# A recommendation tower on one core: row numbers in 3 KB pieces, dense inputs in two transfers, and another order of look-ups

## The reference, cut to what matters

```python
# B=2048 rows, S=16 tables, F=39 fields, D=K=H=16; tables have 1000 to 125000 rows of 16 values
e = stack([tbl_s[ids[:, s]] for s in range(16)], axis=1)               # (2048, 16, 16), look-ups
A  = repeat(r_x0, 16, axis=1)                                          # (2048, 624, 16)
Bm = repeat(e, 39, axis=2).reshape(2048, 624, 16)
z  = einsum('bnh,bnd,nk,khd,kd->bkh', A, Bm, alpha, w, hv).reshape(2048, 256)
h  = concatenate([z, dense_ctx], 1)                                    # dense_ctx (2048, 16)
h  = maximum(h @ W_top1 + b_top1, 0)                                   # 512 wide
h  = maximum(h @ W_top2 + b_top2, 0)                                   # 256 wide
y  = h @ W_top3                                                        # (2048, 1)
```

## Time and profile before

| | us |
|---|---|
| median of 3 runs | 206.6 (205.4 to 207.29) |
| the profiled execution's own time | 207.42 |
| its span in the profile | 205.3 |
| its mean granted PE clock | 0.933 of full speed |

### The profile page before, as it was taken

How to read it: one execution, slowest core, us unless ns; L and a number is a source line. 1 busy time by engine, 2 the same in 40 slices (tenths; PEclk the granted TensorE clock), 3 DMA queues, 4 the chain that set the end, 5 groups by cost and what they waited for, 6 DMA issues and landing times.

```text
span 205.3 us, 5116 instructions
## 1 busy us (share of the span) xinstructions
PE 167.3 (81%) x2170; PEld 123.8 (60%) x2170; DVE 154.7 (75%) x207; ACT 65.5 (32%) x203; POOL 110.4 (54%) x119
## 2 busy tenths in 40 slices
PE   0446993337667999999968999997899899899983
PEld 0446993334354866777746667775577467477671
DVE  3597699159999898998798959888989595595000
ACT  2790018502401136118111451271117318311322
POOL 4777778777777777777777777777500000000000
PEclk9995599556997999999999999999999999999999
DMA  5645589999967999960589999209721960000000
GB/s 123 180 113 131 140 210 224 200 252 203 238 142 155 178 214 182 212 121 10 108 153 211 186 205 188 55 6 200 167 61 38 228 145 2 0 3 0 3 0 2
DMA packets 14098, 26.63 MB, mean 130 GB/s; under 512 B 3932, under 2 KB 11100, under 8 KB 12028
## 3 DMA queue, kind: packets, MB, share of 16 engines
q1 hardware_dynamic: 10156, 25.22, 56.2%
q0 software_dynamic: 3632, 1.06, 4.9%
q10 hardware_dynamic: 288, 0.04, 0.1%
HBM read 26.26 MB, written 0.05 MB: 128 GB/s over the span
## 4 chain that ended last, share of the span: by engine, by line
PE 51%; DVE 21%; DMA 15%; issue 6%; SPq 4%; ACT 1%; DVEq 0%
PE bank L678 15%; DVE prod L585 14%; PE bank L699 13%; PE bank L709 12%; DMA low_h<-low_dram 12%; PE bank L634 5%; DVE onehot L531 4%; PE bank L668 3%; PE bank L693 2%; DMA low_dram<-low 2%; SPq L304 2%; DVE picked L543 2%; DMA prod<-ids_d 1%; SPq L305 1%; DVE prod L487 1%
## 5 line engine op out<-in xcount | busy, mean ns | idle before, releaser
L340 POOL DMA_INDIRECT e_all<-tbl,ids_sb x112 | 109.0, 973 | 35.4 <-issue 33.9
L585 DVE TENSOR_TENSOR prod<-x_main,bank 128x2048 f32<-128x2048 f32 x32 | 72.1, 2278 | 9.2 <-issue 9.2
L678 PE MATMUL bank<-prod,coef 128*32 128x256 f32 x640 | 45.0, 397 | 9.2 <-DVE prod L585 8.5
L634 PE MATMUL bank<-parts,onehot 125*128 125x80 bf16 (+1 forms) x864 | 38.5, 210 | 12.1 <-DVE onehot L531 12.1
L634 PEld LDWEIGHTS bank<-parts,onehot 125*128 125x128 bf16 x864 | 36.4, 107 | 16.9 <-issue 14.9
L411 ACT ACTIVATE spread<-e_all 128x128 f32<-128x128 f32 (+3 forms) x128 | 29.0, 331 | 12.2 <-DMA e_all<-tbl,ids_sb 11.5
L678 PEld LDWEIGHTS bank<-prod,coef 128*32 128x32 f32 x640 | 17.3, 111 | 24.3 <-DVE prod L585 11.6
L699 PE MATMUL bank<-z_sb,w1z_sb 128*128 128x256 f32 x128 | 30.4, 380 | 0.0
L709 PE MATMUL bank<-h_sb,w_sb 128*128 128x256 f32 x128 | 29.8, 386 | 0.7 <-ACT h_sb L421 0.7
L531 DVE TENSOR_SCALAR onehot<-low_h,masks_sb 125x512 bf16<-125x512 f16 x72 | 23.2, 372 | 6.7 <-DMA low_h<-low_dram 6.7
L709 PEld LDWEIGHTS bank<-h_sb,w_sb 128*128 128x128 f32 x128 | 23.7, 190 | 6.9 <-ACT h_sb L421 3.1
(11 more groups left out here) (41 smaller groups left out, 66.1 us busy)
## 6 DMA issues: line engine op xcount, KB each, us to landing
x_main<-x_m SPq DMA_DIRECT2D x16, 512.0 KB, 8.9
x_last<-x_l SPq DMA_DIRECT2D x8, 1024.0 KB
low_h<-low_dram SPq DMA_DIRECT2D x12, 384.0 KB, 8.3
e_all<-tbl,ids_sb POOLq DMA_INDIRECT x112
x_last<-dense_t SPq DMA_DIRECT2D x8, 128.0 KB
prod<-small_tables SPq DMA_DIRECT2D x1, 672.0 KB, 6.3
w1z_sb<-w1z SPq DMA_DIRECT2D x1, 512.0 KB, 16.7
w_sb<-w SPq DMA_DIRECT2D x1, 512.0 KB, 17.1
```

The costliest lines, as they stand in the source:

```text
L340: pool.indirect_dma_start(out=e_all[:, t * E + s * D:t * E + (s + 1) * D], out_offset=None, in_=tables[s], in_offset=bass.IndirectOffsetOn ...
L585: dve.tensor_tensor(prod[:, c, :, :], x0[:, p, :, :], value_bank(g, c // 2)[:, c % 2 * GB:(c % 2 + 1) * GB].unsqueeze(1).broadcast_to([P, ...
L634: last = pe.matmul(look_ps[i % 2][:, t * w:(t + 1) * w], onehot[:, n, c, at:at + P], parts[:, part, col:col + w], start=(t == 0 and c == 0 ...
L678: last = pe.matmul(z_ps[p][32 * q:32 * q + 32, a * GB:(a + 1) * GB], coef[:, c, 4 * a + q, :], prod[:, c, 4 * a + q, :], start=(c == 0 and ...
```

## The change

There are four edits. (1) low_dram is laid out by quarter, so that a transfer of three tables is one run of 3 KB for each partition in place of three of 1 KB; the ids that the digits come from are arranged on the host to match. (2) The twelve dense transfers are two, each of which repeats its source over four partition blocks. The wait for the first row numbers ahead of them is gone, and the row numbers of quarter 1 are issued ahead of x0_last of group 0. (3) Three tables' one-hots (PREFETCH) are made between the first and the second table split, and in the first nine units the one-hots run three ahead of the picks, behind each pick. (4) UNITS_AT is (0, 2, 1, 2, 1, 2, 1) in place of (2, 1, 1, 2, 1, 1, 1).

```diff
--- before.py
+++ after.py
@@ -99,8 +99,9 @@
 RUNS = spread_runs()
 FIRST_COLS = COL0[3]
 LAST_COEF_AT = (2, 4, 6, 8)
-
-UNITS_AT = (2, 1, 1, 2, 1, 1, 1)
+PREFETCH = 3
+
+UNITS_AT = (0, 2, 1, 2, 1, 2, 1)
 LAYER1_AT, LAYER2_AT = (0, 1), 2
 
 
@@ -172,7 +173,7 @@
         low_h = sb("low_h", [P, 2, NSMALL, QUARTER], F16)
         pick = sb("pick", [P, NSMALL * TILES, DMAX])
         picked = sb("picked", [P, 2, QT * DMAX * D])
-        low_dram = nc.dram_tensor("low_dram", [NSMALL, B], F16, kind="Internal").ap()
+        low_dram = nc.dram_tensor("low_dram", [4, NSMALL, QUARTER], F16, kind="Internal").ap()
         alpha_sb = sb("alpha_sb", [P, F8, K])
         w_hv_sb = sb("w_hv_sb", [P, K * H + K])
         wh_sb = sb("wh_sb", [P, K, H])
@@ -198,7 +199,8 @@
         ids_f = early(2 * NSMALL * TILES).rearrange("p (a c) -> p a c", a=2)
         high = early(4 * NSMALL * TILES).rearrange("p (i a c) -> p i a c", i=2, a=2)
 
-        dense_f = [x0_last[:, 1, :, :].rearrange("p h b -> p (h b)")[:, a * HALF:(a + 1) * HALF] for a in range(2)]
+        dense_stage = x0_last[:, 1, :, :].rearrange("p h b -> p (h b)")
+        dense_f = [dense_stage[:, a * HALF:(a + 1) * HALF] for a in range(2)]
         w1d_f = z_sb[:, 0, :, :].rearrange("p a b -> p (a b)")
 
 
@@ -264,7 +266,7 @@
         y_ready = sem("y_ready")
         stored = sem("stored")
 
-        PREP_LOADS, MLP_LOADS, DENSE_LOADS = 2, 4, 12
+        PREP_LOADS, MLP_LOADS, DENSE_LOADS = 2, 4, 2
 
         block = ctx.enter_context(nc.Block())
 
@@ -282,8 +284,9 @@
                 if u >= 2:
                     sp.wait_ge(onehot_ready, 2 * NSMALL * (u - 1))
                 for n in range(0, NSMALL, 3):
-                    sp.dma_start(low_h[:, u % 2, n:n + 3, :], low_dram[n:n + 3, u * QUARTER:(u + 1) * QUARTER].unsqueeze(0).broadcast_to(
-                        [P, 3, QUARTER])).then_inc(low_in[u % 2][n // 3], 16)
+                    sp.dma_start(low_h[:, u % 2, n:n + 3, :].rearrange("p n b -> p (n b)"),
+                                 low_dram[u, n:n + 3, :].rearrange("n b -> (n b)").unsqueeze(0).broadcast_to(
+                                     [P, 3 * QUARTER])).then_inc(low_in[u % 2][n // 3], 16)
 
             sp.wait_ge(low_stored, 16)
             load_low(0)
@@ -296,16 +299,11 @@
                 sp.dma_start(x0_last[:, p, :, :], x0_l[g].unsqueeze(1).broadcast_to(
                     [2 * 8, J, HP * GB])).then_inc(last_in[p], 16)
 
-            for n in range(NSMALL // 3):
-                sp.wait_ge(low_in[0][n], 16)
-            for q in range(4):
-                rows = slice(32 * q, 32 * q + 32)
-                for a in range(2):
-                    sp.dma_start(dense_f[a][rows, :], dense_t[:, a * HALF:(a + 1) * HALF]).then_inc(dense_in, 16)
-                sp.dma_start(w1d_f[rows, :], w1d).then_inc(dense_in, 16)
+            sp.dma_start(dense_stage, dense_t.unsqueeze(0).broadcast_to([4, 32, B])).then_inc(dense_in, 16)
+            sp.dma_start(w1d_f, w1d.unsqueeze(0).broadcast_to([4, 32, N1])).then_inc(dense_in, 16)
             load_main(0, 0)
+            load_low(1)
             load_last(0, 0)
-            load_low(1)
             load_main(1, 1)
             sp.dma_start(w1z_sb[:, :, :], w1z.rearrange("(a p) n -> p a n", p=P)).then_inc(mlp_in, 16)
             sp.dma_start(w2_sb[:, :, :], w2.rearrange("(a p) n -> p a n", p=P)).then_inc(mlp_in, 16)
@@ -384,7 +382,7 @@
                 last.then_inc(coef_done, 1)
 
             act.wait_ge(low_ready, 1)
-            act.dma_start(low_dram.rearrange("n b -> (n b)").rearrange("(p c) -> p c", p=P), low16[:, :]).then_inc(low_stored, 16)
+            act.dma_start(low_dram.rearrange("u n b -> (u n b)").rearrange("(p c) -> p c", p=P), low16[:, :]).then_inc(low_stored, 16)
             spread_weights()
             spread_sums()
 
@@ -557,14 +555,15 @@
             dve.wait_ge(table_in, 16)
             split_tables(0, slice(0, FIRST_COLS))
             dve.wait_ge(split_step, 4)
+            for n in range(PREFETCH):
+                make_onehot(n)
             split_tables(1, slice(FIRST_COLS, W))
-            make_onehot(0)
             dve.wait_ge(pick_ready, 1)
             dve.wait_ge(low_ready, 1)
             for n in range(NSMALL):
-                if n < NSMALL - 1:
-                    make_onehot(n + 1)
                 pick_rows(n)
+                if n + PREFETCH < NSMALL:
+                    make_onehot(n + PREFETCH)
             split_dense()
             for i in units_at(0):
                 make_onehot(i)
@@ -765,7 +764,7 @@
     rows_to = lambda a, n: _np.concatenate([a, _np.zeros((n - a.shape[0],) + a.shape[1:], a.dtype)], 0)
     arrays = {
         "ids": flat(ids.reshape(TILES, P, S).transpose(1, 0, 2)),
-        "ids_d": flat(_np.stack([flat(hot.T).reshape(P, NSMALL * TILES),
+        "ids_d": flat(_np.stack([hot.T.reshape(NSMALL, 4, QUARTER).transpose(1, 0, 2).reshape(P, NSMALL * TILES),
                                  hot.reshape(TILES, P, NSMALL).transpose(1, 2, 0).reshape(P, NSMALL * TILES)], 1)),
         **{f"tbl_{s}": flat(tables[f"tbl_{s}"]) for s in GATHERED},
         "x0_m": flat(x0[:, :, 0:FM]).reshape(GROUPS, 2 * FM, HP * GB),
```

## The result

The changed kernel takes 217.08 us against 206.94 for the one before (medians of 4 executions), a ratio of 1.050 (95% interval 1.040 to 1.060). The forecast was 204.3 and "faster" or "same"; the change made it 5% slower. The profiled execution took 219.35 us (span 217.2), 2.3 above its median. Executions in a second, slower state stand outside the ratios: this one is counted there (1.6% above the fastest), and so are, among others, one of e2_tiled at 250.0 us and one of e5_oldunits at 246.4, both with a mean granted clock of about 0.66.

The account below looks back on a forecast made before the run. The front was taken to wait for quarter 1's row numbers, with PE and DVE alternating as the bound behind it. The sum -5.9 + 1.05 + 0.55 + 1.0 + 1.0 = -2.3 us gave a 204.3 us median, range 200.8 to 207.0.

Parts of the forecast that it names:

- step 0: Front up to the first product: it would start at 38.7 in place of 44.60, with quarter 1's row numbers landed in time.
- the split beside the spread: DVE's dense split during ACT's first spread: 3.8 us, done at 37.7 and off the path.
- 3 KB runs: First row-number piece lands at 14.4 in place of 15.6; if the longer runs bring nothing, the sum is 1.2 us less.
- Edit 3 costs 0.7 us: DVE's new front order: last pick ends at 33.8 against 33.15, in spite of the earlier row numbers.
- Gain 5.9 us at step 0: The first product starts at 38.7 in place of 44.60.
- The steps give back 3.6 us: Losses from the new look-up spread: 1.05 and 0.55 in groups 0 and 1, 1.0 for each of two later pairs.
- Rival D: Group 0's gathers queue behind bulk DMA and delay ACT's first spread to about 40; sum +3.7, 210.3 us; chance 0.11.
- D's second half: Group 1's gathers, wanted by 51.4 for ACT's spread; each microsecond beyond is lost in full.
- Rival B: New look-up spread costs nothing in later groups and PE's clock is back early in front; 200.7 us; chance 0.20.
- C: PE's full clock comes 3 us later in front and step 0 runs longer at half clock; 206.7 us; chance 0.14.

Follow-up runs that it names:

- e2_tiled: The changed kernel with the dense inputs as two transfers of 128 distinct rows, tiled on the host; 204.58 us, ratio 0.991.
- e5_oldunits: The changed kernel with eight dense transfers and the earlier UNITS_AT (2, 1, 1, 2, 1, 1, 1); 198.77 us, ratio 0.968.
- a4: The changed kernel's two repeated dense transfers (leading dimension 4), with SP waits before and behind so only gathers run beside; 22.6 us from weights' issue to next issue.
- e1_eight: The changed kernel with the dense inputs in eight transfers of 32 partitions in place of two repeated ones; 202.73 us, ratio 0.981.
- e8_3kb: The kernel before with the 3 KB row numbers alone changed; 201.65 us, ratio 0.982.
- e9_repeat: The kernel before with its twelve dense transfers replaced by the two repeated ones, wait and order kept; 224.15 us in one execution.
- e6_oldfront: The changed kernel with eight dense transfers and the earlier front order of table split and one-hots on DVE; 203.56 us, ratio 0.989.
- e7_oldboth: The changed kernel with eight dense transfers, earlier DVE front order and earlier UNITS_AT, so only the transfers differ from the kernel before; 198.92 us, ratio 0.968.
- e4_wait: The changed kernel with SP's wait for the first three row-number transfers put back ahead of the repeated dense transfers; 222.96 us.
- e3_two: The changed kernel with the two dense transfers repeating a 64-row source twice (leading dimension 2); 218.73 us.

## Why the prediction was wrong

**The step that failed** is in the part on step 0: "4.72 MB at 221 GB/s", and "the dense values come to ACT sooner, which nobody waits for". Both took the two dense transfers at the rate of all 16 engines. They ran on four (a4), and took 34.6 us from issue to landing in the changed kernel. What SP queued behind them was late too: the longest transfer of row numbers landed 35.6 us after its issue, against 16.9. And somebody does wait: ACT's program has round_dense ahead of the first spread. I had named the cover (the split beside the spread) but not the price if it went. None of the three rivals was this. I had counted the edit as fewer issues of the same bytes and not asked how a transfer is shared out. The order rows showed only the destination, 128 partitions; the source's four by 32 stood in the diff.

The Trainium skill has the rule (DMA: Bandwidth & Descriptors, Why a DMA increments its semaphore by 16 and not by 1): a transfer gets the largest number of engines, up to 16, that divides the slowest dimension (of those larger than 1) of both sides, which is 4 here. The trace agrees: 25.6% and 25.0% of 16 engines with a leading 4, 12.6% with a leading 2, and 76.9% from 16 to 20 us with 128 rows, whose start and end lie in that stretch.

**With that step mended, the sum held, in part by luck.** The kernel with 128 distinct rows differs from the changed one in nothing else:

| step | forecast, us | two transfers of distinct rows, us |
|---|---|---|
| first row numbers, from the store's landing | 4.2 | 3.6 |
| last pick ends | 33.8 | 33.7 |
| first product, group 0 | 38.7 | 38.76 |
| first product, group 1 | 60.5 | 60.19 |
| contraction (1, 1) | 67.6 | 67.26 |
| first product, group 4 | 118.9 | 118.89 |
| contraction (5, 1) | 149.3 | 148.89 |
| time | 205.1 for the profiled one, 204.3 median | 204.74 and 204.58 |

The rows of the table's first products (DVE, kernel with distinct rows), against the earlier trace rows:

```profile
38.76 2.29 DVE L584 TENSOR_TENSOR prod<-x_main,bank 128x2048 f32<-128x2048 f32 x1 [1.25 <-PE bank L667]
...
60.19 2.27 DVE L584 TENSOR_TENSOR prod<-x_main,bank 128x2048 f32<-128x2048 f32 x1
...
118.89 2.29 DVE L584 TENSOR_TENSOR prod<-x_main,bank 128x2048 f32<-128x2048 f32 x1 [4.14 <-issue]
```

and of its contractions (PE), against the earlier trace rows:

```profile
67.26 1.07 PE L677 MATMUL bank<-prod,coef 128*32 128x256 f32 x16 [0.65 <-DVE prod L584]
```
```profile
148.89 1.07 PE L677 MATMUL bank<-prod,coef 128*32 128x256 f32 x16 [0.46 <-DVE prod L584]
```

In this kernel's own trace the first product comes 5.8 us sooner than before and the steps give back 3.2 (158.63 - 38.76 against 161.32 - 44.60), so 2.7 are left (204.74 against 207.42), where the forecast had 5.9, 3.6 and 2.3. By medians it is 1.6 us (204.58 against 206.21, ratio 0.991). Two agreements are better than the reasoning behind them. The last pick is on time because two misses cancel: look-up 2 began at 19.13, 1.5 sooner than the 20.6 of the prediction, and PE's granted clock was still at 0.50 from 24 to 28 us and 0.75 from 28 to 32, where the kernel before had 0.73 and 1.00. And group 4's first product falls on the forecast with a break of 1.24 us of PE in it (at 108 us), of the kind seen in e1_eight, which the forecast did not have.

Point by point:

- **3 KB runs** (taken as 1.2 us for the first piece): between 1.5 and 1.8. The bound of 13.9 was reached. The Trainium skill's rule that 512 B suffice for line rate (DMA: Bandwidth & Descriptors, Specifications), weighed in the prediction, is not borne out here: with the 3 KB runs alone changed (e8_3kb) the fastest piece took 3.8 us from issue to landing, against 5.4 and 5.2 in e9_repeat with 1 KB runs.
- **Edit 3 costs 0.7 us**: neither confirmed nor refuted. With 3 KB runs the last pick ended at 29.9, 31.8 and 33.0 in the three traces with the old order (e8_3kb, e6_oldfront, e7_oldboth), the latter two with PE standing still for 1.42 and 2.45 us in a look-up. With the new order it ended anywhere from 29.9 to 36.4, later the longer PE ran at half speed in the front. In e4_wait, the latest, eight coefficient matmuls at 30.49 still took 1.87 us; at 28.59 in the changed kernel, the earliest, they took 1.04. (In e4_wait PEclk reads 1.00 there, so the length of the rows is the better witness.)
- **Gain 5.9 us at step 0**: 5.8 (44.60 to 38.76).
- **The steps give back 3.6 us**: 3.9 by the traces of e1_eight and e5_oldunits, which differ in UNITS_AT alone. The parts fit less well than the sum: 0.7 in groups 0 and 1, where I had 1.6; 2.3 in groups 2 and 3, where I had 1.0, with PE's break of 1.30 in it; and 0.85 in groups 4 and 5, where I had 1.0.
- **Rival D** (gathers): with the last pick at 31.8 or later, group 0's gathers were in time, e.g. with the spread at 32.16 right behind the last pick in e1_eight. With the last pick at 29.9 they were not: in e8_3kb the spread waited 3.0 us longer for a gather, to 32.95, where the prediction had them landed by 31.5. In that trace picks that ended earlier gained nothing at the spread. D's second half did show as a wait without cost: group 1's spread starts at 50 to 51 behind its gathers, as before. **Rival B** is refuted by what the new spread costs. **C**: in the kernel with distinct rows PE's clock did come back late in the front, as said above; the earlier start had paid for it.

## What to carry to other kernels

Before two transfers replace twelve, look at the slowest dimension of the source and of the destination: a broadcast with a leading 4 turns a 16-engine transfer into a 4-engine one, slow for itself and for all that its queue holds. Then ask what else the engine that waits for it has in its stream: a wait that cost nothing when it ended at 30 us held DVE for 18 when it ended at 45. And split a change of four edits into its parts: here the 3 KB runs and the other edits to the transfers, with eight for the dense inputs, gained 6.9 us together (205.85 to 198.92), the new order in the front nothing that shows, the new spread of look-ups lost 4 to 4.6, and the four-engine source lost 12.5 (against distinct rows) to 14.4 (against eight transfers). By medians 4.2 of the 6.9 belong to the 3 KB runs alone (e8_3kb, 201.65), but by the lower two of its four executions 5.9 do, so that split is not firm.

## What the runs showed of the hardware

- While the queue ran on two engines, the DMA engines looked idle as a whole (DMA share 0.20, 60 GB/s), and SP was still held at its next issues for 20.7 us (e3_two). What holds it is not shown.
- With only gathers beside them, an engine moved an 8 KB packet in 0.31 us when two were used, in 0.50 to 0.54 when four were, and with sixteen in 0.33 (128 distinct rows) or 0.53 (eight rows repeated 16 times). Open.
- 384 KB from DRAM to 128 partitions in 1 KB runs had landed after 5.2 to 5.4 us, in 3 KB runs after 3.6 to 3.9.
- In several kernels PE stood still in the middle of one contraction or look-up, and the trace shows nothing that ended it (1.30 us at 105.4 in e1_eight, 1.70 at 122.1 in the changed kernel, 2.45 at 27.3 in e7_oldboth). Open.
- PEclk can miss a stretch at half clock: in e4_wait it reads 1.00 from 16 to 32 us, while eight coefficient matmuls took 1.87 us at 20.75, 25.62 and 30.49 and 1.04 at 35.16.
